# Expert weights of a mixture-of-experts layer on one Trainium2 core: three whole transfers per expert, or twelve of 32 partitions

## The chip, the core and the metric

The kernel runs on one core of one Trainium2 chip. The metric is the device time of one execution in microseconds. Durations of single instructions and stretches come from one profiled execution, whose times are counted from the start of its span.

## What is computed

One pre-norm transformer layer over 8 sequences of 512 tokens (4096 tokens of width 512). The first part is attention, half softmax attention and half a gated linear recurrence. The second part, which the change touches, is a mixture of 32 experts with a capacity of 160 slots each. Cut to what matters:

```python
C = int(math.ceil(CF * T / E))                   # 160 slots per expert
slots_token = jnp.zeros(EC, jnp.int32).at[dest].add(jnp.where(valid, tok_s, 0))
slots_w = jnp.zeros(EC, w_s.dtype).at[dest].add(jnp.where(valid, w_s, 0.0))
Xp = x[slots_token].reshape(E, C, d)             # E = 32, d = 512
G = jnp.einsum('ecd,edi->eci', Xp, W_gate)       # i = 256
U = jnp.einsum('ecd,edi->eci', Xp, W_up)
Y = jnp.einsum('eci,eid->ecd', jax.nn.silu(G) * U, W_down)
Yf = Y.reshape(EC, d) * slots_w[:, None]
out = jnp.zeros((T, d), x.dtype).at[slots_token].add(Yf)
return (out + shared).reshape(b, s, d)
```

Each expert has three float32 matrices of 512 KB: gate and up (512 x 256) and down (256 x 512).

## The kernel before, in words

The program has three phases, one behind the other.

**Attention** (to about 2077 us) doesn't meet the change.

**Routing and shared expert** (to about 2446 us) goes over eight blocks of 512 tokens. It picks the experts, scatters each token's row into a table `rows` in HBM with one indirect transfer per 128 tokens and pick (L1306, POOL), and writes the shared expert's result into the output. SP stores a block (L1268), loads the next one (L1238), and ahead of the store of block 5 issues the weights of the first five experts (L1262 to L1266), which nothing there needs yet.

**Experts** (`expert_phase`, from 2446 us) goes over the 32 experts. Each engine's order is written out by hand:

- SP loads the input rows of an expert (`load_x`, L1802: 160 rows of 528 values, on 80 partitions, into one of four tiles `xg`) and its weights (`load_expert`, L1099, into one of five sets of `held.room`). Weights of expert e + 1 wait until DVE has converted all three matrices of the expert that had the set before (`w_low`); inputs of expert e wait until PE has turned and POOL has read the expert that had the tile (`turned`, `share_ready`, L1800 and L1801).
- ACT converts gate, up and down to a high fp16 part (`up_high` L1855, `down_high` L1862), DVE to a low part (L1905). PE turns the inputs (L1952), multiplies by gate and up (L1965) and by down (L1978), each as three products of high and low parts.
- ACT scales the result by the slot's weight into one of four tiles `yo` (`copy_down`, L1881). POOL prepares that weight (`weigh`, L1822 to L1831) and adds the 160 rows to the output with two indirect accumulating transfers (`add`, L1840). Ahead of the two stands a wait until the previous expert's two have landed:

```python
for e in range(E_):
    if e + 2 < E_:
        weigh(e + 2)
    add(e)
```

```python
pool.wait_ge(share_ready, e + 1)
if e:
    pool.wait_ge(added, ONE_ADD * e)
pool.wait_ge(yo_ready, n_ct * (e + 1))
```

A weight matrix is laid on 128 partitions of 4 KB each, contiguous in HBM. All transfers but the indirect ones are issued by SP. The instructions that the change touches are `load_expert` and the two waits in `up_high` (L1856) and `down_high` (L1863).

Of the kernel before, what the change touches and what calls it, by code (L numbers as in the profile page):

```python
# [6 lines left out]
P = 128  # L7
# [1057 lines left out]
AT_SLOTS = AT_WEIGHTS + K  # L1065
ROW = DM + 16
SETS = 5


class Held:  # L1070


    def __init__(self, nc, ctx, cap):
        n_ct, ct = slot_tiles(cap)

        def sb(name, shape, dt=F32):
            return ctx.enter_context(nc.sbuf_tensor("held_" + name, shape, dt))

        self.room = sb("expert_w", [P, SETS, 3, DC * FF])
        self.ident = sb("ident", [P, P])  # L1080
        self.own = sb("own", [ct, n_ct, E_])
        self.up_loaded = [ctx.enter_context(nc.semaphore(f"expert_up_loaded{n}")) for n in range(SETS)]
        self.down_loaded = [ctx.enter_context(nc.semaphore(f"expert_down_loaded{n}")) for n in range(SETS)]

# [9 lines left out]
    def tail_room(self, n):  # L1094
        flat = self.room[:, SETS - 2:SETS, :, :].rearrange("p n m w -> p (n m w)")
        return flat[:, n * 4 * DM:(n + 1) * 4 * DM].rearrange("p (r d) -> p r d", d=DM)


def load_expert(eng, held, w_gate, w_up, w_down, e):  # L1099

    n = e % SETS
    eng.dma_start(held.gate(n), w_gate[e].rearrange("(p c) i -> p c i", p=P)).then_inc(held.up_loaded[n], 16)
    eng.dma_start(held.up(n), w_up[e].rearrange("(p c) i -> p c i", p=P)).then_inc(held.up_loaded[n], 16)
    eng.dma_start(held.down(n), w_down[e].rearrange("(p c) d -> p c d", p=P)).then_inc(held.down_loaded[n], 16)


def routing_phase(nc, x2, router_w, e_bias, shared_gate, shared_up, shared_down, consts, acc_dram, rows_dram, held,
# [10 lines left out]
    with ExitStack() as ctx:  # L1118
# [117 lines left out]
        def _(sp):  # L1236
# [25 lines left out]
            for b in range(B):  # L1262
                if b == max(B - 3, 0):
                    sp.wait_ge(w_ready, 12)
                    for e in range(SETS):
                        load_expert(sp, held, w_gate, w_up, w_down, e)  # L1266
                sp.wait_ge(summed, NT * (b + 1))
                sp.dma_start(acc_dram[b * SEQ:(b + 1) * SEQ, :].rearrange("(i p) d -> p i d", p=P), xr[b % RING][:]).then_inc(base_stored, 16)  # L1268
                if b + RING < B:
                    sp.wait_ge(base_stored, 16 * (b + 1))  # L1270
                    load_x(b + RING)
# [465 lines left out]
def expert_phase(nc, T, w, rows_dram, acc_dram, out, held):  # L1737
# [5 lines left out]
    w_gate, w_up, w_down = w  # L1743
    out_rows = out.rearrange("b t d -> (b t) d")
    with ExitStack() as ctx:
# [26 lines left out]
        def by_chunk(bank):  # L1772
            return bank[:, 0:FC * cap].rearrange("p (c t) -> p c t", c=FC)
# [22 lines left out]
        @block.sync  # L1796
        def _(sp):
            def load_x(e):
                if e >= XS:
                    sp.wait_ge(turned, n_ct * (e - XS + 1))  # L1800
                    sp.wait_ge(share_ready, e - XS + 1)  # L1801
                sp.dma_start(xg[e % XS][:], rows_dram[e * cap:(e + 1) * cap, :].rearrange("(j p) d -> p j d", p=ct)).then_inc(x_loaded[e % XS], 16)  # L1802

            for e in range(XS):
                load_x(e)
            for e in range(XS, E_):
                if e + 1 >= SETS and e + 1 < E_:
                    sp.wait_ge(w_low, 3 * (e + 1 - SETS + 1))
                    load_expert(sp, held, w_gate, w_up, w_down, e + 1)
                load_x(e)  # L1810
            sp.wait_ge(added, ONE_ADD * E_)
# [39 lines left out]
        @block.scalar  # L1851
        def _(act):
            act.preload_act_table_set("sigmoid_and_others")

            def up_high(e):  # L1855
                act.wait_ge(held.up_loaded[e % SETS], 32 * (e // SETS + 1))  # L1856
                if e >= 2:
                    act.wait_ge(up_done, e - 1)
                for whole, part in ((held.gate(e % SETS), wg_part), (held.up(e % SETS), wu_part)):
                    nc.scalar.activation(part[e % 2][0][:], whole, ACT.Copy, scale=W_SCALE).then_inc(w_high, 1)  # L1860

            def down_high(e):  # L1862
                act.wait_ge(held.down_loaded[e % SETS], 16 * (e // SETS + 1))  # L1863
                if e >= 2:
                    act.wait_ge(down_done, n_ct * (e - 1))
                nc.scalar.activation(wd_part[e % 2][0][:], held.down(e % SETS), ACT.Copy, scale=W_SCALE).then_inc(w_high, 1)

            def copy_turned(e):
                for j in range(n_ct):
                    act.wait_ge(turned, n_ct * e + j + 1)  # L1870
                    nc.scalar.activation(xp_t[e % 2][0][:, :, j * ct:(j + 1) * ct],
                                         tr_ps[j % 2][:, 0:DC * ct].rearrange("p (c t) -> p c t", c=DC),
                                         ACT.Copy, scale=X_SCALE).then_inc(x_high_ready, 1)

            def copy_down(e):
                act.wait_ge(share_ready, e + 1)
                if e >= XS:
                    act.wait_ge(added, ONE_ADD * (e - XS + 1))
                for j in range(n_ct):
                    act.wait_ge(down_done, n_ct * e + j + 1)  # L1880
                    nc.scalar.activation(yo[e % XS][:, j, :], down_ps[j % 2][0:ct, :], ACT.Copy,  # L1881
                                         scale=share[e % XS][:, j:j + 1]).then_inc(yo_ready, 1)

            up_high(0)
            copy_turned(0)
            for e in range(E_):
                down_high(e)
                if e + 1 < E_:
                    up_high(e + 1)
                    copy_turned(e + 1)  # L1890
                act.wait_ge(gate_done, e + 1)
                if e >= 2:
                    act.wait_ge(h_step, 2 * (e - 1))
                nc.scalar.activation(sig[e % 2][:], by_chunk(gate_ps[e % 2]), ACT.Sigmoid,
                                     scale=1.0 / (X_SCALE * W_SCALE)).then_inc(sig_ready, 1)
                if e:
                    copy_down(e - 1)
                act.wait_ge(h_step, 2 * (e + 1))
                nc.scalar.copy(h_part[e % 2][0][:], h[e % 2][:]).then_inc(h_high_ready, 1)
            copy_down(E_ - 1)  # L1900
# [172 lines left out]
```

## Time and profile before, and how to read it

| | |
|---|---|
| median of 3 runs | 2734.24 us (2732.66 to 2735.64) |
| the profiled execution | 2731.19 us |
| its span, first to last instruction | 2729.2 us |
| PE busy | 2533.8 us, 93% of the span |
| DVE, ACT, POOL busy | 1918.4, 1574.0, 1565.8 us |
| DMA, mean over the span | 52 GB/s, 143.23 MB |
| routing phase / expert phase | about 2077 to 2446 / 2446 to 2729 us |

The busy shares are means over three phases that have different limits; the change bears on the last 283 us and on a stretch from 2327 us. For that phase the views by stretch and by wait are the ones to read.

### The profile page before, as it was taken

The numbers are of one execution on the slowest core, as the hardware profiler recorded it, in microseconds if no ns is written. First come the engines' busy times: TensorE is split into PE (matmuls) and PEld (weight loads), VectorE is DVE, ScalarE is ACT, GpSimd is POOL, SyncE is SP. The second block draws the span as 40 slices with busy tenths as digits, with TensorE's granted clock in tenths as the row PEclk, the third lists the DMA queues.
The fourth block names the chain that finished last, engine by engine and source line by source line (L and its number), as shares of the span: only waits on it lengthen the run. The fifth ranks groups of instructions, "written<-read, shape, count | busy, mean of one in ns | idle before, by whom it ended". The sixth has DMA issues, their size and how long they took to land. (4 is left out here: it accounts for less than half of the span.)

```text
span 2729.2 us, 52852 instructions
## 1 busy us (share of the span) xinstructions
PE 2533.8 (93%) x16740; PEld 1729.4 (63%) x16740; DVE 1918.4 (70%) x4613; ACT 1574.0 (58%) x4789; POOL 1565.8 (57%) x2005
## 2 busy tenths in 40 slices
PE   5899999999999999999999999999996899979885
PEld 3666666666666666666666666666664444538764
DVE  7777677767776776777777777766764777647763
ACT  5656666666665655666666656655654333317664
POOL 4556556655665565566556655655541566655665
PEclk8999999999999999999999999999998999989998
DMA  5500000000000000000000000000003221427783
GB/s 177 191 1 17 30 3 1 17 32 1 2 17 32 1 17 17 17 1 17 32 1 2 17 32 1 2 5 28 1 1 113 91 80 36 165 60 257 258 254 73
DMA packets 68767, 143.23 MB, mean 52 GB/s; under 512 B 15863, under 2 KB 21239, under 8 KB 68304
## 3 DMA queue, kind: packets, MB, share of 16 engines
q1 hardware_dynamic: 52112, 128.39, 13.9%
q0 software_dynamic: 16384, 11.47, 2.2%
q8 instruction: 141, 2.31, 0.4%
q14 instruction: 130, 1.06, 0.1%
HBM read 111.60 MB, written 72.68 MB: 68 GB/s over the span
## 5 line engine op out<-in xcount | busy, mean ns | idle before, releaser
L303 POOL TENSOR_TENSOR parts<-qk,rope 128x640 f32<-128x640 f32 x128 | 197.4, 1542 | 441.2 <-issue 301.3
L437 ACT ACTIVATE prob<-score_ps,neg_max 128x512 f32<-128x512 f32 (+3 forms) x512 | 272.2, 532 | 249.7 <-DVE neg_max L630 213.2
L857 PE MATMUL out_ps<-prob_t,val 128*128 128x512 f32 (+3 forms) x1024 | 305.6, 442 | 14.4 <-ACT prob_t L443 10.3
L830 PE MATMUL score_ps<-kr_t,qr_t 128*128 128x512 f16 (+3 forms) x1536 | 284.1, 300 | 13.2 <-ACT prob L437 11.2
L638 DVE TENSOR_SCALAR prob<-prob,inv_sum 128x512 f32<-128x512 f32 (+3 forms) x512 | 273.5, 534 | 18.0
L857 PEld LDWEIGHTS out_ps<-prob_t,val 128*128 128x128 f32 x1024 | 185.2, 191 | 134.0 <-issue 62.1
L630 DVE TENSOR_REDUCE neg_max<-score_ps 128x1 f32<-128x512 f32 (+3 forms) x512 | 237.2, 483 | 25.9 <-PE score_ps L832 19.7
L479 ACT ACTIVATE soft<-qk,neg_top 128x128 f32<-128x128 f32 x640 | 247.1, 387 | 0.8
L343 POOL TENSOR_TENSOR k_dec<-decay,keys 128x32 f32<-128x32 f32 (+3 forms) x512 | 165.5, 355 | 83.1 <-ACT decay L499 83.1
L315 POOL TENSOR_TENSOR rot<-parts 128x320 f32<-128x320 f32 x128 | 110.9, 866 | 167.8 <-DVE parts L660 167.8
L636 DVE RECIPROCAL inv_sum<-row_sum 128x1 f32<-128x1 f32 x512 | 81.1, 158 | 175.5 <-ACT prob L437 175.4
L903 PE MATMUL qkv_ps<-wq_high,x_t_high 128*128 128x512 f16 x512 | 197.0, 385 | 2.0 <-DVE wkv_low L561 2.0
L903 PE MATMUL qkv_ps<-wq_low,x_t_high 128*128 128x512 f16 x512 | 196.9, 384 | 0.0
L903 PE MATMUL qkv_ps<-wq_high,x_t_low 128*128 128x512 f16 x512 | 196.7, 384 | 0.0
L356 POOL TENSOR_TENSOR o_t_low<-parts,o_t_high 128x512 f16<-128x512 f32 x128 | 148.1, 1157 | 75.1 <-ACT parts L453 75.1
L830 PEld LDWEIGHTS score_ps<-kr_t,qr_t 128*128 128x128 f16 x1536 | 135.5, 98 | 82.8 <-ACT prob L437 38.5
L321 POOL TENSOR_TENSOR soft<-soft,inv_tot 128x512 f32<-128x512 f32 x128 | 146.1, 1141 | 63.3 <-DVE inv_tot L672 63.3
L462 ACT ACTIVATE qk<-qkv_ps 128x640 f32<-128x640 f32 x128 | 90.1, 704 | 142.4 <-issue 127.7
L443 ACT COPY prob_t<-prob_ps 128x384 f32<-128x384 f32 (+1 forms) x256 | 94.6, 369 | 116.3 <-DVE prob_t L646 114.2
L1306 POOL DMA_INDIRECT rows<-r_yn,r_sk_i x128 | 129.2, 1009 | 53.8 <-issue 45.7
L1840 POOL DMA_INDIRECT out_dram<-e_yo,e_goal x64 | 107.7, 1683 | 89.5 <-issue 73.7
L332 POOL TENSOR_TENSOR decay<-keys 128x512 f32<-128x512 f32 x128 | 141.5, 1106 | 7.8 <-ACT keys L486 5.8
(294 smaller groups left out, 7807.2 us busy)
## 6 DMA issues: line engine op xcount, KB each, us to landing
held_expert_w<-in_L_ffn_W_gate_dram SPq DMA_DIRECT2D x32, 512.0 KB
held_expert_w<-in_L_ffn_W_up_dram SPq DMA_DIRECT2D x32, 512.0 KB
held_expert_w<-in_L_ffn_W_down_dram SPq DMA_DIRECT2D x32, 512.0 KB
rows<-const_empty_dram SPq DMA_DIRECT2D x1, 10560.0 KB, 39.7
e_xg<-rows SPq DMA_DIRECT2D x32, 330.0 KB, 4.9
x_in<-_attn_hidden_states_dram SPq DMA_DIRECT2D x8, 1024.0 KB, 5.5
x_acc<-_attn_hidden_states_dram SPq DMA_DIRECT2D x8, 1024.0 KB, 5.4
x<-x_acc SPq DMA_DIRECT2D x8, 1024.0 KB, 4.4
```

Of the source, the lines that this page charges most:

```text
L303: nc.gpsimd.tensor_tensor(parts[:, 1, :].rearrange("p (h d) -> p h d", d=HALF), qk[:].rearrange("p (h d) -> p h d", d=HALF), rope[:, i, 1: ...
L321: nc.gpsimd.tensor_tensor(q, q, inv_tot[:, 0:G].unsqueeze(2).to_broadcast([P, G, DH]), ALU.mult).then_inc(soft_query_ready, 1)
L332: nc.gpsimd.tensor_tensor(decay[:, 0:NSUB * P].rearrange("p (c s) -> p c s", s=P), mid.to_broadcast([P, NSUB, P]), run.unsqueeze(1).to_bro ...
L343: ins = nc.gpsimd.tensor_tensor(k_dec[:, s, 0:m], decay[:, s * P:s * P + m], keys[:, 0:m], ALU.mult)
L356: nc.gpsimd.tensor_tensor(o_t[1][:, h, :], o_whole, o_t[0][:, h, :], ALU.subtract).then_inc(o_t_ready, 1)
L437: nc.scalar.activation(prob[:, i % 2, 0:w], score_ps[i % 2][:, 0:w], ACT.Exp, bias=neg_max[:, j:j + 1], accum_out=row_sum[:, j:j + 1]).the ...
L479: ins = nc.scalar.activation(soft[:, h * DH:(h + 1) * DH], qk[:, h * DH:(h + 1) * DH], ACT.Exp, bias=neg_top[:, h:h + 1], accum_out=tot[:, ...
L630: nc.vector.tensor_reduce(neg_max[:, j:j + 1], score_ps[i % 2][:, 0:w], AX_X, ALU.max, negate=True).then_inc(max_ready, 1)
L638: nc.vector.tensor_scalar(prob[:, i % 2, 0:w], prob[:, i % 2, 0:w], inv_sum[:, j:j + 1], None, ALU.mult).then_inc(prob_ready, 1)
L830: nc.tensor.matmul(score_ps[i % 2][:, 0:w], qr_t[p][:, q_, h, i * P:(i + 1) * P], kr_t[p][:, k_, 0:w], start=(n == 0), stop=False)
L857: nc.tensor.matmul(out_ps[:, j * P:SEQ], val[p][:, j, :], prob_t[:, j, j * P:SEQ], start=(j == 0), stop=False, skip_group_check=True)
L903: ins = nc.tensor.matmul(qkv_ps[:, 0:G * DH], x_t[x_part][:, d, i * P:(i + 1) * P], wq[w][:, d, gn * G * DH:(gn + 1) * G * DH], start=(d = ...
```

## The change

Each of an expert's three transfers becomes four, of 32 partitions and 128 KB each. The pieces of gate and up alternate: gate 0, up 0, gate 1, up 1, and so on, and the four pieces of down follow. The semaphores `up_loaded` and `down_loaded` of a set now rise by 128 and 64 for one expert instead of 32 and 16, and the two waits of ACT ask for these sums. All of an expert's pieces are issued behind the same wait as before.

```diff
+PIECES = 4
...
 def load_expert(eng, held, w_gate, w_up, w_down, e):
 
     n = e % SETS
-    eng.dma_start(held.gate(n), w_gate[e].rearrange("(p c) i -> p c i", p=P)).then_inc(held.up_loaded[n], 16)
-    eng.dma_start(held.up(n), w_up[e].rearrange("(p c) i -> p c i", p=P)).then_inc(held.up_loaded[n], 16)
-    eng.dma_start(held.down(n), w_down[e].rearrange("(p c) d -> p c d", p=P)).then_inc(held.down_loaded[n], 16)
+    for q in range(PIECES):
+        at = slice(q * P // PIECES, (q + 1) * P // PIECES)
+        eng.dma_start(held.gate(n)[at], w_gate[e].rearrange("(p c) i -> p c i", p=P)[at]).then_inc(held.up_loaded[n], 16)
+        eng.dma_start(held.up(n)[at], w_up[e].rearrange("(p c) i -> p c i", p=P)[at]).then_inc(held.up_loaded[n], 16)
+    for q in range(PIECES):
+        at = slice(q * P // PIECES, (q + 1) * P // PIECES)
+        eng.dma_start(held.down(n)[at], w_down[e].rearrange("(p c) d -> p c d", p=P)[at]).then_inc(held.down_loaded[n], 16)
...
             def up_high(e):
-                act.wait_ge(held.up_loaded[e % SETS], 32 * (e // SETS + 1))
+                act.wait_ge(held.up_loaded[e % SETS], 32 * PIECES * (e // SETS + 1))
...
             def down_high(e):
-                act.wait_ge(held.down_loaded[e % SETS], 16 * (e // SETS + 1))
+                act.wait_ge(held.down_loaded[e % SETS], 16 * PIECES * (e // SETS + 1))
```

The order of SP's instructions in the middle of the expert phase, before (one expert's weights, the next input load, and the first weight of the following expert; `e_xg` is the input tile, 80x2x528 its partitions and row):

```order
L1102 DMA held_expert_w<-in_L0_ffn_W_gate_dram 128x1024 [waits e_w_low]
L1103 DMA held_expert_w<-in_L0_ffn_W_up_dram 128x1024
L1104 DMA held_expert_w<-in_L0_ffn_W_down_dram 128x1024
L1802 DMA e_xg1<-rows 80x2x528 [waits e_share_ready,e_turned]
L1102 DMA held_expert_w<-in_L0_ffn_W_gate_dram 128x1024 [waits e_w_low]
```

The same place of the changed program:

```order
L1105 DMA held_expert_w<-in_L0_ffn_W_gate_dram 32x1024 [waits e_w_low]
L1106 DMA held_expert_w<-in_L0_ffn_W_up_dram 32x1024
L1105 DMA held_expert_w<-in_L0_ffn_W_gate_dram 32x1024
L1106 DMA held_expert_w<-in_L0_ffn_W_up_dram 32x1024
L1105 DMA held_expert_w<-in_L0_ffn_W_gate_dram 32x1024
L1106 DMA held_expert_w<-in_L0_ffn_W_up_dram 32x1024
L1105 DMA held_expert_w<-in_L0_ffn_W_gate_dram 32x1024
L1106 DMA held_expert_w<-in_L0_ffn_W_up_dram 32x1024
L1109 DMA held_expert_w<-in_L0_ffn_W_down_dram 32x1024 x4
L1807 DMA e_xg0<-rows 80x2x528 [waits e_share_ready,e_turned]
L1105 DMA held_expert_w<-in_L0_ffn_W_gate_dram 32x1024 [waits e_w_low]
```

Between two input loads there are now twelve issues instead of three. The same holds in the routing phase, where sixty issues stand in front of the store of block 5 instead of fifteen. No instruction of the other engines moves.

## Rows read from the trace of the kernel before

**Rows 1.** The chain that ended last, in order of time: start, duration, what.
```profile
2714.45 1.42 DMA out_dram<-e_yo,e_goal
...
2720.93 1.42 POOL out_dram L1840
```

**Rows 2.** Waits, 2504 to 2670: waited for, us in total, times, longest.
```profile
POOL out_dram L1840 <- issue: 53.6, 40, 5.5
ACT e_yo L1881 <- POOL e_goal L1831: 41.4, 16, 3.7
```

**Rows 3.** POOL in order of time: scatters at the stretch's ends and the last.
```profile
2468.42 1.50 POOL L1840 DMA_INDIRECT out_dram<-e_yo,e_goal  x1 [10.18 <-ACT e_yo L1881]
...
2506.80 1.50 POOL L1840 DMA_INDIRECT out_dram<-e_yo,e_goal  x1 [5.55 <-issue]
...
2672.20 1.64 POOL L1840 DMA_INDIRECT out_dram<-e_yo,e_goal  x1 [3.66 <-issue]
...
2712.71 1.43 POOL L1840 DMA_INDIRECT out_dram<-e_yo,e_goal  x1 [3.35 <-issue]
...
2719.21 1.42 POOL L1840 DMA_INDIRECT out_dram<-e_yo,e_goal  x1 [3.35 <-issue]
```

**Rows 4.** The output's scatters, 2504 to 2672: issue to landing.
```profile
DMA to landing us min/median/max: 3.8/5.8/7.5
```

**Rows 5.** The same from 2676 us to the end.
```profile
DMA to landing us min/median/max: 2.5/3.9/5.0
```

**Rows 6.** Stretches: length, busy PE PEld DVE ACT POOL (instructions), clock, DMA share, GB/s.
```profile
2330.00:2350.00 20.00, 19.72 (x114) 11.06 (x115) 17.69 (x57) 11.23 (x20) 15.55 (x16) 0.91 1.04 403
2448.00:2452.00 4.00, 1.34 (x8) 1.10 (x8) 3.29 (x4) 2.85 (x5) 2.05 (x4) 0.50 1.04 253
...
2504.00:2664.00 160.00, 144.08 (x1379) 115.27 (x1377) 113.16 (x161) 108.77 (x181) 104.55 (x154) 0.99 0.80 249
```

**Rows 7.** SP in order of time: issues of weights and inputs.
```profile
2327.82 0.50 SPq L1102 DMA_DIRECT2D held_expert_w<-in_L_ffn_W_gate_dram  x1
...
2333.80 1.48 SPq L1104 DMA_DIRECT2D held_expert_w<-in_L_ffn_W_down_dram  x1
...
2363.50 78.41 SPq L1268 DMA_DIRECT2D out_dram<-r_xr  x3
...
2453.76 0.36 SPq L1102 DMA_DIRECT2D held_expert_w<-in_L_ffn_W_gate_dram  x1
...
2585.97 0.33 SPq L1802 DMA_DIRECT2D e_xg<-rows  x1
2586.34 0.44 SPq L1102 DMA_DIRECT2D held_expert_w<-in_L_ffn_W_gate_dram  x1
...
2587.31 0.43 SPq L1104 DMA_DIRECT2D held_expert_w<-in_L_ffn_W_down_dram  x1
```

**Rows 8.** What SP's queue waited for, 2504 to 2670.
```profile
SPq L1801 <- POOL e_goal L1831: 124.9, 20, 8.9
```

**Rows 9.** The router weights' transfer, 32 partitions, 64 KB: issue ns.
```profile
L1242 SPq DMA_DIRECT2D r_rw<-in_L_ffn_router_w_dram x1: 423/423/423, 2079.2 to 2079.2; - x1
```

**Rows 10.** ACT in order of time: first expert, and the last one.
```profile
2447.50 1.06 ACT L1860 ACTIVATE e_wg_high<-held_expert_w 128x1024 f16<-128x1024 f32 x1
...
2687.41 1.05 ACT L1860 ACTIVATE e_wg_high<-held_expert_w 128x1024 f16<-128x1024 f32 x1
...
2697.59 1.26 ACT L1881 ACTIVATE e_yo<-e_down_ps,e_share 80x512 f32<-80x512 f32 x2 [2.44 <-POOL e_goal L1831]
2698.75 0.45 ACT L1899 CAST e_h_high<-e_h 128x320 f16<-128x320 f32 x1
```

**Rows 11.** DMA issues of the page: KB each, median us to landing.
```profile
e_xg<-rows SPq DMA_DIRECT2D x32, 330.0 KB, 4.9
```

**Rows 12.** PE in order of time: first and last matmul of a down product.
```profile
2591.32 0.38 PE L1978 MATMUL e_down_ps<-e_wd_high,e_h_high 128*80 128x512 f16 x1
...
2593.69 0.38 PE L1978 MATMUL e_down_ps<-e_wd_high,e_h_low 128*80 128x512 f16 x1
```

## Prediction

> **What bounds the kernel now.** The change touches only the transfers of the expert weights, so I read the expert phase alone (from 2446 us) and asked what sets the pace of one expert there. First the end: the chain that ended last is the accumulating scatter into the output, the landing of one (2714.45) and then the issue of the next (2720.93), with nothing of the matrix engine in it [rows 1]. Then the waits of the steady stretch 2504 to 2670 us: POOL stands 53.6 us in front of its scatters (L1840) although no engine is named, and ACT stands 41.4 us in front of `yo` for the shares that POOL writes [rows 2]. In the code POOL waits at that place for the previous expert's scatters to have landed (`added`). Nobody in that stretch waits for weights. Third, POOL in order of time [rows 3]: the first scatter of one expert starts at 2506.80 and that of the expert twenty later at 2672.20, so one expert takes 165.4 / 20 = 8.27 us. At the end, with no weights in flight, two such starts (2712.71 and 2719.21) are 6.50 us apart. The difference is the landing: issue to landing has a median of 5.8 us in the stretch with weight traffic and 3.9 us behind it [rows 4, 5]. So the expert phase is a chain of 32 experts' scatters, and the DMA traffic beside them sets its pace.
>
> Fourth, the DMA engines by stretch [rows 6]. Five experts' weights, all on 128 partitions, move in 2330 to 2350 at 403 GB/s with the engines fully busy (share 1.04; above 1, packets overlap). In 2448 to 2452 the queue holds the first expert inputs, which have 80 partitions, and the engines are as busy (1.04) but move only 253 GB/s. That is the row this forecast rests on: 253 / 403 = 0.63, and 80 / 128 is 0.63. In the steady stretch the share is 0.80. Last, SP [rows 7]: an expert is one input issue and three weight issues, at a pitch of 0.48 us, and SP then waits 124.9 / 20 = 6.2 us per expert for POOL [rows 8].
>
> **The change, part by part.**
>
> *Issues.* Three issues per expert become twelve; nine more at the pitch of 0.485 us (2586.34 to 2587.31, two steps [rows 7]) are 4.4 us, out of the 6.2 us that SP waits. A 32-partition transfer of before was issued in 423 ns [rows 9], no cheaper and no dearer than a 128-partition one. SP then needs 12 x 0.485 + 0.37 = 6.2 us of 8.27 us: free. Behind these issues on SP stands the next input load (L1802), which lands 4.4 us later at worst; by the code its tile is used two experts (16 us) later. Free as well. The semaphore sums change from 32 and 16 to 128 and 64 per round, with the same waits at the same places of ACT.
>
> *Prefetch in the routing phase.* Sixty issues (29 us) from 2327.82; SP is next wanted at 2363.50 [rows 7]. 7.86 MB take 20 us at 403 GB/s and 39 us at half of it, until 2367 us, and the first use is at 2447.5 [rows 10]: covered by 80 us. POOL's row scatters run beside it for longer; between 0 and 3 us, I take 0.
>
> *The rate of a piece.* All of it hangs on this. A piece writes 32 partitions where a whole transfer wrote 128; bytes and row size (4 KB) are the same. No large 32-partition transfer is in the trace, so I bound it. At one end the partitions don't matter: 403 GB/s, 1.573 MB in 3.9 us per expert. At the other the rate falls with the number of partitions, as it does between 128 and 80: 403 / 4 = 101 GB/s, 15.6 us. I take half, 202 GB/s and 7.8 us, the geometric middle; the row at 80 partitions excludes for me that nothing happens, and a load in which sixteen engines still take part is unlikely to fall to a quarter.
>
> The Trainium skill (SBUF — State Buffer, Door 1: The DMA port swizzle) says that a transfer reaches only the ports its own partitions belong to, 8 of 16 for partitions 0 to 31, and gives 189 GB/s at 1 MiB and about 218 GB/s at best; by it the weights of one expert would be an estimated 7.2 to 8.3 us. By that rule 80 partitions reach full width only for a part of their bytes, with which the 253 GB/s agree. The same page's "Can I just issue two DMAs to hit both halves?" says that pieces on different halves gain only 6% from each other, which speaks against this change.
>
> *DMA demand per expert.* Weights 7.8 us. The input, 0.338 MB (330 KB, [rows 11]) at 253 GB/s, 1.35 us. The scatters: now 0.80 x 8.27 = 6.6 us of engine time per expert, less 3.9 and 1.35, leaves 1.35, say 1.4 us. Sum 7.8 + 1.35 + 1.4 = 10.5 us, above the 8.27 us of today: the DMA engines become the pace.
>
> *Where that ends.* From the weights' side: the first load in the expert phase is issued at 2453.76 [rows 7]; 27 experts at 10.5 us are 284 us; from the last landing to the end I count 24 us: 11.3 from the last expert's first conversion to its product (2687.41 to 2698.75), less the 2.4 in which ACT waited for POOL, the down product 2.7 (2591.32 to 2593.69, and one matmul), `yo` 1.3 [rows 10, 12], 10.0 from its first scatter to the end, and 1 for the landing. 2453.8 + 283.5 + 24 = 2761 us, 32 us over the span of 2729.2. From the scatters' side: first scatter at 2468.42 [rows 3], 27 steps at 10.5, four at 6.5 behind the last weights, 10.0 from the last expert's first scatter to the end: 2468.4 + 283.5 + 26 + 10 = 2788 us, 59 us over. The scatter chain starts slow if the weights don't hold it up yet, so I take the middle, **+45 us**. Time of the profiled execution 2731.19 + 45 = 2776; it lies 3.05 below the median of the three runs, so against those it is **2780 us**.
>
> Bounds of the same term. At 403 GB/s the sum is 3.9 + 1.35 + 1.4 = 6.65 us, below 8.27: nothing. At 253 GB/s, 8.95 us: 27 x 0.68 = +18 us. From the landing: weight traffic at a share of 0.80 costs 5.8 - 3.9 = 1.9 us; if it is always there, and each piece in the way takes twice as long, 1.9 / 0.80 x 2 = 4.75 us on top of 6.50, a step of 11.25 us and 2468.4 + 304 + 36 = 2808 us, +79.
>
> **The rivals.**
>
> *The pieces move as fast as before.* Then weights are landed some 20 us before use as now, SP has room, and the time stays at 2734. For it: the sixteen engines may drift apart, so that some write one piece and some the next; the bytes are the same. Against: the 80-partition row. Chance 0.15.
>
> *Faster: the issues pace the traffic.* This needs the rate to stay near 403 GB/s. Today three issues put 1.57 MB into the queue in 1.5 us, and a scatter that meets it lands up to 7.5 us later [rows 4]. Twelve issues spread the same bytes over 5.8 us, 270 GB/s, leaving a third of the engines free at any moment; the 1.9 us of delay would shrink by a third, 20 steps x 0.6 = -12 us, 2722 us. It decides once pieces run above about 270 GB/s. The Trainium skill (Perfetto Trace Analysis, DMA Optimizations) says that splitting may let transfers start sooner where the DMA engines are generally idle; here they are busy for 0.80 of the time. Chance 0.08.
>
> *SP becomes the bound.* With a full queue issues took up to 1.48 us each [rows 7]. At about 1.1 us for each piece, an expert is 12 x 1.1 + 0.37 = 13.6 us: 2453.8 + 367 + 24 = 2845, about 2850 us. Against: those slow issues drained 512 KB each, pieces are a quarter. Chance 0.05.
>
> *The rate falls to a quarter.* 15.6 + 2.75 = 18.3 us per expert: 2453.8 + 494 + 24 = 2972, about 2977 us. Chance 0.07.
>
> That the change doesn't split at all is excluded: the instruction order shows pieces of 32 partitions.
>
> **How the numbers follow.** The forecast case, slower by 10 to 95 us around 2780, has 0.65. No change 0.15, faster 0.08, the two dear cases 0.12. The measurement can tell about 0.2%, 5.5 us. Faster by more than that 0.08, within it 0.15, slower 0.65 + 0.12 = 0.77. The range leaves out the fast rival and the two dear ones, 0.20 together: from 2729, the no-change case's lower edge, to 2830, the +79 bound and some 15 us for a slower drain. The forecast's own range is 2745 to 2830.
>
> **What would show it.** In the changed profile: the stretch 2330 to 2350 at about 200 GB/s with a share of 1.0, the weights landing past 2360; in the expert phase a share near 1.0 and less than 230 GB/s; a step of 10 us or more between experts' first scatters; ACT waiting for weight transfers at L1865; scatter landing median 7 us or more. I am wrong if 2330 to 2350 still shows 400 GB/s, or if it shows 200 and the expert phase still keeps 8.3 us, which would mean that the scatters' landing, not the engines' capacity, is what matters. SP waiting for nothing at all would be the third rival.

## The result, and the profile after

The change makes the kernel slower: 2765.16 us (median of 4 runs, 2763.88 to 2766.46) against 2733.66 us (4 runs), a ratio of 1.0119 with a 95% interval of 1.0106 to 1.0132, or +31.5 us. 2780 was forecast, with a range of 2729 to 2830. The profiled execution has a span of 2764.4 us, 35.2 more than before.

One stretch of the prefetch, before:

```profile
2338.00:2350.00 12.00, 12.00 (x58) 6.06 (x58) 11.13 (x47) 6.76 (x12) 8.75 (x9) 0.86 1.04 399
```

The same stretch of the kernel after, and one of its expert phase (columns as in [rows 6]):

```profile
2338.00:2350.00 12.00, 12.00 (x73) 7.47 (x72) 11.21 (x37) 6.03 (x11) 8.10 (x8) 1.00 1.06 230
2504.00:2664.00 160.00, 131.23 (x1195) 103.69 (x1193) 96.73 (x137) 91.91 (x153) 83.24 (x136) 0.95 1.01 223
```

In the prefetch the DMA engines are as busy as before (1.06) and move 230 GB/s instead of 399. The last row answers to 0.80 and 249 GB/s: in the expert phase the engines are now busy all the time and bring fewer bytes, and PE's busy time falls from 144 to 131 us of 160.

POOL in order of time, the scatters that open an expert's step:

```profile
2471.04 1.50 POOL L1845 DMA_INDIRECT out_dram<-e_yo,e_goal  x1 [10.40 <-ACT e_yo L1886]
...
2506.73 1.76 POOL L1845 DMA_INDIRECT out_dram<-e_yo,e_goal  x1 [5.32 <-issue]
...
2698.14 2.51 POOL L1845 DMA_INDIRECT out_dram<-e_yo,e_goal  x1 [5.07 <-issue]
...
2754.48 1.41 POOL L1845 DMA_INDIRECT out_dram<-e_yo,e_goal  x1 [3.29 <-issue]
```

From 2506.73 to 2698.14 are twenty steps, from the fourth expert to the 24th: 9.57 us each. The same twenty steps took 8.36 us before. The 8.27 us of [rows 3] are those from the fifth expert to the 25th, and these take 9.41 us now. The span's 35.2 us can be read off these times. The first scatter is 2.6 us late. Most of that is older than the change, since the first weight issue already comes 2.4 us later than before (2330.19 against 2327.82, [rows 7]). From the first scatter to the fourth expert's it is 35.7 us against 26.4 (+9.3), over the next twenty steps 191.4 against 167.3 (+24.1), and over the last eight, of which only the first still has weights beside it, 56.3 against 57.1 (-0.8). In the first stretch, 2465 to 2504 us, the median landing of the scatters is 9.4 us where it was 5.1, so the early steps lose by the same wait.

The waits of the same stretch as in [rows 2], 2504 to 2690 us, and below them what SP's queue waited for:

```profile
POOL out_dram L1845 <- issue: 89.8, 39, 7.0
ACT e_yo L1886 <- POOL e_goal L1836: 76.4, 19, 6.4
DVE e_h_low L1946 <- ACT e_h_high L1904: 62.0, 20, 5.6
```

```profile
SPq L1806 <- POOL e_goal L1836: 58.9, 19, 5.6
```

The same waits as before have grown: POOL in front of its scatters, ACT for POOL's shares. No row names a weight transfer. SP still waits for POOL, 3.1 us per expert where it was 6.2 [rows 8]. The landing of the scatters, 2504 to 2700 us:

```profile
DMA to landing us min/median/max: 4.5/6.8/9.9
```

5.8 has become 6.8 us [rows 4]. Behind the weight traffic the median is 3.9 us in both.

### The profile page after: what moved, and what is told of

Read it like the earlier page. It is cut to its first block and busy times, and to the rows that moved or that the text cites. A ratio compares the mean times of both kernels' runs of the same rounds, so it can differ in the third digit from the quotient of the medians.

```text
span 2764.4 us, 53140 instructions
## 1 busy us (share of the span) xinstructions
PE 2551.7 (92%) x16740; PEld 1739.5 (63%) x16740; DVE 1918.7 (69%) x4613; ACT 1571.8 (57%) x4789; POOL 1552.9 (56%) x2005
## 5 line engine op out<-in xcount | busy, mean ns | idle before, releaser
L499 ACT ACTIVATE decay<-decay 128x640 f32<-128x640 f32 x128 | 96.6, 754 | 85.0 <-POOL decay L335 85.0
```

## The experiments

All are built on the changed kernel unless said otherwise. Each was built to tell between theories. Theory A: a transfer's rate depends on which partitions it writes, and 32 neighbours reach half the width. B: the number of transfers costs. C: the number of partitions in a transfer sets its rate. D: the step grows with the slow transfers smoothly, against a threshold of the engines' capacity.

### Every fourth partition

```diff
-        at = slice(q * P // PIECES, (q + 1) * P // PIECES)
+        at = slice(q, P, PIECES)
```

> Twelve pieces of 32 partitions and 4 KB rows as in the change, but piece q takes partitions q, q+4, q+8 and so on over all 128. Theory A (a piece of neighbouring partitions reaches only half of the write width): the prefetch stretch moves 380 to 400 GB/s again instead of 227, the step between experts' first scatters is 7.8 to 8.4 us instead of 9.57, the time 2722 to 2740 us. Theory B (the number of transfers costs, by their fixed work on the engines) and theory C (the number of partitions in one transfer sets its rate): 227 GB/s, 9.6 us, about 2765 us.

Measured: 2736.23 us (2732.9 to 2742.73), ratio 1.0015 (1.0006 to 1.0024). Its prefetch stretch, and SP's issues of gate:

```profile
2338.00:2350.00 12.00, 12.00 (x65) 7.00 (x64) 11.18 (x37) 5.90 (x10) 8.57 (x9) 0.86 0.71 208
```

```profile
L1105 SPq DMA_DIRECT2D held_expert_w<-in_L_ffn_W_gate_dram x128: 468/594/1752, 2329.5 to 2685.8; - x128
```

The time is what A expected, the rate is not: 208 GB/s. But the engines are busy for only 0.71 of it, where the change's pieces had them at 1.06 for 230 GB/s. What limits here is the issue, 594 ns a piece instead of 422: 131 KB in about 0.64 us are 205 GB/s. So the same bytes, rows and count of pieces take clearly less engine time once a piece is spread over all partitions, and B and C fall. They are not as cheap as whole transfers: 0.71 for 208 GB/s is 31% more engine time per byte than 1.04 for 399. The issue shows in the expert phase too, 2504 to 2664 us:

```profile
PEld e_tr_ps L1957 <- DMA e_xg<-rows: 22.8, 15, 3.5
PE e_tr_ps L1957 <- DMA e_xg<-rows: 19.8, 14, 3.3
```

PE waits for inputs, which stand behind the twelve issues on SP, and SP itself has no wait left in that stretch. The scatters land in 5.0 us (the row below, 2504 to 2664 us), but SP's twelve issues set a step of 8.30 us (fifth expert to 25th). The third rival of the prediction happens here, in another kernel than the one it was for.

```profile
DMA to landing us min/median/max: 3.2/5.0/6.8
```

### Two halves

```diff
-PIECES = 4
+PIECES = 2
```

> Two pieces per matrix, partitions 0 to 63 and 64 to 127, six transfers per expert. Theory A: each still reaches half the width, so 220 to 235 GB/s in the prefetch and about 2765 us. Theory B: half of the added transfers, so half of the loss of time per byte, about 290 GB/s and 2745 to 2750 us. Theory C: twice the partitions of a piece, clearly above 227 GB/s (about 300), 2740 to 2750 us.

Measured: 2765.45 us, ratio 1.0114 (1.0099 to 1.0130), that is the changed kernel's time.

```profile
2338.00:2350.00 12.00, 12.00 (x66) 7.06 (x65) 11.18 (x38) 5.90 (x10) 8.45 (x9) 0.86 1.05 233
```

64 neighbouring partitions move at 233 GB/s and 32 at 230. Half the number of transfers gains nothing (against B), twice the partitions gain nothing (against C). Whole transfers on 128 move at 403.

The Trainium skill (SBUF — State Buffer, Door 1: The DMA port swizzle) gives 189 GB/s for partitions 0 to 31 and 196 for 0 to 63 at 1 MiB; by that rule, 8 ports of 16 for both, the runs agree in the equality, and lie some 20% above its figures. They also lie 6% over the 218 GB/s that the prediction quotes from it as the best.

### The order of the sides

Three runs change nothing but the order of the twelve pieces.

```diff
-    for q in range(PIECES):
+    for q in (0, 2, 1, 3):
```

> The twelve pieces of the change, issued in the order of partitions 0-31, 64-95, 32-63, 96-127, so that pieces that follow each other lie on different sides of partition 64 (gate and up of the same partitions still follow each other). Theory A, if the engines overlap pieces that follow each other: above 227 GB/s, 240 to 300, and 2745 to 2760 us; if they keep step: 227 GB/s and 2765 us. Theories B and C: 227 GB/s and 2765 us.

The second issues the four pieces of gate, then the four of up, in order:

```diff
     for q in range(PIECES):
         at = slice(q * P // PIECES, (q + 1) * P // PIECES)
         eng.dma_start(held.gate(n)[at], ...
+    for q in range(PIECES):
+        at = slice(q * P // PIECES, (q + 1) * P // PIECES)
         eng.dma_start(held.up(n)[at], ...
```

> The pieces of the change, but the four of gate first, then the four of up: two pieces below partition 64 are followed by two above, instead of four by four. The alternation of gate and up itself is worth nothing since nobody waits for weights. Theory A with overlap of neighbours: a gain from the more frequent change of side as in the run with the order 0, 2, 1, 3, which had the same pattern for gate and up, 2748 to 2756 us. Without overlap: 2765 us.

The third does both, so that every piece is followed by one from the other side of partition 64.

> Gate, then up, then down, each in the order 0-31, 64-95, 32-63, 96-127: every piece is followed by one on the other side of partition 64. Theory A with overlap: more overlap than with pairs, 260 GB/s or more in the prefetch, 2735 to 2748 us. If the 2750 us of the pairs was the most that overlap gives: 2750 us.

Measured: 2749.6 us (ratio 1.0065, 1.0049 to 1.0081), 2757.53 (1.0093, 1.0078 to 1.0108) and 2743.59 (1.0038, 1.0024 to 1.0053). The prefetch stretch of the first, the second and the third:

```profile
2338.00:2350.00 12.00, 12.00 (x50) 5.15 (x49) 11.28 (x38) 5.09 (x9) 9.70 (x9) 0.89 1.06 243
```

```profile
2338.00:2350.00 12.00, 12.00 (x69) 6.81 (x69) 11.14 (x47) 6.82 (x12) 8.43 (x10) 1.00 1.05 232
```

```profile
2338.00:2350.00 12.00, 12.00 (x67) 6.58 (x67) 11.11 (x48) 7.01 (x12) 8.70 (x9) 1.00 1.06 251
```

The more often the side of partition 64 changes, the lower the time (2765, 2758, 2750, 2744). The rate rises from 230 to 243 and 251 GB/s in the first and third; in the second, where the side changes only every two pieces, it is 232. What differs is the order of the pieces, so A holds once more, and neighbours on the queue overlap a little, 9% at most. The rates of the last run fell short of the 260 expected; the time was inside. The second run was put a little too low (2748 to 2756); I had left out that its down pieces keep their order. The alternation of gate and up, which is what it undoes, costs some 6 or 7 us of the 31.5 (1.0119 against 1.0093, with intervals that just meet); with it four pieces in a row write the same side.

### Cut by columns

```diff
-        eng.dma_start(held.gate(n)[at], w_gate[e].rearrange("(p c) i -> p c i", p=P)[at]).then_inc(held.up_loaded[n], 16)
+        eng.dma_start(held.gate(n)[:, q, :], w_gate[e].rearrange("(p c) i -> p c i", p=P)[:, q, :]).then_inc(held.up_loaded[n], 16)
```

(up and down likewise, each piece 128 partitions by 1 KB.)

> Twelve pieces of 128 KB per expert, each on all 128 partitions with a row of 1 KB instead of 4 KB (the matrices cut by columns of the tile). Theory A: 330 to 400 GB/s in the prefetch and 2730 to 2745 us, the small loss by the shorter rows. Theory B: 227 GB/s or less and 2765 us or more. Theory C: as A.

Measured: 2734.28 us (10 runs), ratio 1.0003 (0.9994 to 1.0013): no loss.

```profile
2338.00:2350.00 12.00, 12.00 (x66) 7.07 (x65) 11.18 (x39) 6.61 (x11) 8.14 (x9) 0.86 0.92 282
```

282 GB/s is below the 330 expected. A piece was issued in 432 ns; with the gap between issues that is about 0.47 us, which allows 279 GB/s: here too SP paces the prefetch. Twelve transfers per expert as such cost no time: B falls for good. They do occupy the engines longer, 0.93 of the expert phase instead of 0.80.

One rival to A was not tested. A matrix's row lies in HBM where its partition says, so every piece of neighbouring partitions also reads one contiguous block of HBM, and the strided and column pieces read from all over the matrix. What speaks against HBM as the cause is that pieces taken in turn from two matrices on the same side moved no faster (230 GB/s, the change) than pieces from one (232 GB/s, gate and then up), while a change of side did raise the rate.

### Part of the weights only

Down alone in pieces (gate and up whole, their wait sum 32 again):

```diff
+    eng.dma_start(held.gate(n), ...).then_inc(held.up_loaded[n], 16)
+    eng.dma_start(held.up(n), ...).then_inc(held.up_loaded[n], 16)
     for q in range(PIECES):
         ... held.down(n)[at] ...
```

> Only the down matrix goes in four pieces of 32 neighbouring partitions; gate and up go whole. Theory A with the engines' capacity as the pace (a step takes the sum of the engine time of an expert's weights, input and scatters): 2 x 1.3 + 2.3 + 1.35 + 1.4 = 7.6 us, below today's 8.27, so no loss, 2731 to 2738 us. Rival D (the scatters land later in proportion to how long slow pieces are under way, whatever the sum): a third of the loss, about +10 us, 2743 us.

Gate and up alone in pieces, down whole (its wait sum 16 again):

```diff
     for q in range(PIECES):
         ... held.gate(n)[at] ... held.up(n)[at] ...
+    eng.dma_start(held.down(n), ...).then_inc(held.down_loaded[n], 16)
```

> Only gate and up go in pieces, down goes whole. Capacity: 4.6 + 1.3 + 1.35 + 1.4 = 8.65 us, 0.4 above 8.27, so 27 x 0.4 = +10, 2740 to 2748 us. Rival D: two thirds of the loss, +21 us, 2754 us.

The pieces for the first five experts alone (`if e < SETS:`, whole transfers behind it):

> The pieces of the change for the first five experts alone, which are loaded in the routing phase; all later ones whole. If the routing phase covers the slow loads as forecast: 2731 to 2738 us. If the slow prefetch costs something itself (row scatters of POOL held up, store of block 5 behind sixty issues): up to the whole 32 us.

Measured: down alone 2741.69 us, ratio 1.0042 (1.0029 to 1.0056), +11.5; gate and up alone 2756.24, 1.0092 (1.0078 to 1.0105), +26; prefetch alone 2731.41, 1.0002 (0.9993 to 1.0011). The expert phase of the first, and the landing of its scatters:

```profile
2504.00:2664.00 160.00, 138.66 (x1283) 111.61 (x1282) 104.56 (x150) 100.18 (x166) 98.20 (x151) 0.96 0.88 238
...
DMA to landing us min/median/max: 2.9/6.1/8.1
```

Slow pieces in the prefetch are free, as forecast, though they fill the engines there:

```profile
2338.00:2350.00 12.00, 12.00 (x65) 7.04 (x64) 11.21 (x38) 6.84 (x11) 8.14 (x9) 0.86 1.06 230
```

In the expert phase there is no threshold for such pieces. With down alone the engines have 12% of their time free and the sum I had taken as the pace lies under 8.27 us, yet 11.5 us are lost, a good third of the whole. Rival D holds (it gave 2743 and 2754 us), and the capacity rule falls.

### Less traffic

From the kernel before, with the weight transfers of experts 5 to 31 cut to a row of 512 B:

```diff
+    eng.dma_start(held.gate(n)[:, 0, 0:FF // 2], ...[:, 0, 0:FF // 2]).then_inc(held.up_loaded[n], 16)
```

> The kernel before, whose weight transfers in the expert phase (experts 5 to 31) bring only one eighth of each matrix, a row of 512 B on all 128 partitions; the rest of the weights is left out. It shows the pace of the scatter chain with hardly any weight traffic. If the traffic sets the landing as I say: scatters land in about 4 us instead of 5.8, the step falls from 8.27 to 6.9 to 7.4 us, the time to 2700 to 2712 us. If the chain has a pace of its own: above 2725 us.

From the changed kernel, pieces with half of each row for experts 5 to 31:

```diff
-        eng.dma_start(held.gate(n)[at], ...[at]).then_inc(held.up_loaded[n], 16)
+        eng.dma_start(held.gate(n)[at, 0:2], ...[at, 0:2]).then_inc(held.up_loaded[n], 16)
```

> The twelve pieces of the change with only the first half of each row (2 KB) for experts 5 to 31; the other half of these weights is left out. The bytes are half, the engine time of an expert's weights is 786 KB / 227 GB/s = 3.5 us, near the 3.9 us of the whole transfers. Theory D' (the scatters' delay follows the time for which weight transfers occupy the engines): as before, 2723 to 2732 us. If it follows the bytes: halfway between the eighth (2706) and before, 2714 to 2720 us. If it follows the lower rate as such (each packet of a piece in the way takes twice as long): 2745 us or more.

Measured: 2705.67 us (0.9911, 0.9896 to 0.9926) and 2719.33 us (0.9952, 0.9937 to 0.9967). Both leave weights out and are no improvements. First the run with an eighth, then the one with half rows:

```profile
2504.00:2664.00 160.00, 159.40 (x1569) 130.44 (x1567) 130.68 (x185) 129.72 (x207) 131.75 (x178) 1.00 0.45 92
...
DMA to landing us min/median/max: 2.6/4.0/5.1
```

```profile
2504.00:2664.00 160.00, 152.44 (x1480) 122.25 (x1478) 124.19 (x176) 119.04 (x195) 122.03 (x167) 1.00 0.71 165
...
DMA to landing us min/median/max: 2.6/4.5/6.5
```

With an eighth of the weights the step falls to 7.24 us and 24.5 us come back: the weights cost the kernel before 24.5 us by delaying the scatters, though nobody waits for them. The scatters are no longer what sets the pace in that run. PE is busy 159.4 of 160 us, and POOL stands only 23.0 us in front of 44 scatters (53.6 us for 40 before), so still earlier landings would gain little. The half-row run came out at -12.5 us, in the range of "follows the bytes", and refuted the third reading, by which the low rate itself would double each delay (2745). It doesn't separate the other two: I had put the engine time of its weights 0.4 us below that of whole transfers (3.5 against 3.9), but its share of 0.71 over a step of 7.82 us is 5.6 us per expert, about 1 below the kernel before (0.80 x 8.27 = 6.6), so less time was occupied as well. Bytes alone can't be the rule all the same, since the change moves the same bytes as before and lost 31.5 us. With the measured shares, engine time per expert and time of the kernel go together:

| pieces | share x step, us | landing, us | time against before, us |
|---|---|---|---|
| an eighth of the weights | 0.45 x 7.24 = 3.3 | 4.0 | -24.5 |
| half rows | 0.71 x 7.82 = 5.6 | 4.5 | -12.5 |
| before | 0.80 x 8.27 = 6.6 | 5.8 | 0 |
| every fourth partition | 0.86 x 8.30 = 7.1 | 5.0 | +3 |
| columns | 0.93 x 8.33 = 7.7 | 5.5 | +1 |
| gate and up every fourth, down whole (below) | 0.93 x 8.21 = 7.6 | 5.4 | +2 |
| down alone | 0.88 x 8.62 = 7.6 | 6.1 | +11.5 |
| sides in turn | 0.95 x 8.48 = 8.1 | 5.8 | +12 |
| gate and up alone | 0.99 x 9.09 = 9.0 | 6.3 | +26 |
| two halves | 1.00 x 9.45 = 9.45 | 7.1 | +32.5 |
| the change | 1.01 x 9.41 = 9.5 | 6.7 | +31.5 |

(The step is the mean from the fifth expert's first scatter to the 25th's; share and landing are those of 2504 to 2664 us; the time is against the runs of before beside it.) Two cautions. Where the share is 1, share times step is the step itself, so those rows don't show by how much engine time delays a scatter. And the landing column leaves out the steps ahead of 2504 us, where from a third to over a half of the loss lies: from the first expert to the fifth the change lost 9.8 us, sides in turn 6.6, down alone 6.1, columns 3.2.

The runs whose pieces lie on all partitions stand out, by columns and with gate and up on every fourth: as much engine time as with down alone, and next to no loss. The scatters read `yo` on partitions 0 to 79; whether slow pieces on the same side as these hold them up more than others was not tried, and stays open.

### A try to gain from it

The strided run had the scatters land in 5.0 us and failed by SP's issues. With gate and up so cut and down whole (its wait sum 16 again) SP has room:

```diff
-        at = slice(q * P // PIECES, (q + 1) * P // PIECES)
+        at = slice(q, P, PIECES)
...
+    eng.dma_start(held.down(n), w_down[e].rearrange("(p c) d -> p c d", p=P)).then_inc(held.down_loaded[n], 16)
```

> Gate and up in four pieces each of every fourth partition, down whole: nine issues per expert. In the run with all three matrices cut that way SP never waited and its twelve issues of 594 ns set the step (8.38 us) while the scatters landed in 5.0 us. Here SP needs 8 x 0.64 + 0.48 + 0.37 = 6.0 us and has room again. If the scatter chain then profits from the paced traffic: landing about 5.2 us, step 7.7 to 7.9, 2718 to 2728 us. If the landing goes by the bytes alone: 2730 to 2736 us.

Measured: 2733.78 us (12 runs), ratio 1.0011 (1.0003 to 1.0020). That is in the range of "by the bytes alone", and not in that of a gain. The landing fell to 5.4 us and SP waits 36.5 us again, but the step stayed at 8.21 us. Why the earlier landing gained nothing is open. No version with all the weights beat the kernel before.

```profile
2504.00:2664.00 160.00, 146.56 (x1401) 118.00 (x1399) 114.07 (x161) 109.38 (x181) 110.95 (x159) 0.98 0.93 257
```

## Why the prediction was right, and where it was not

**What bounds the kernel: right.** The chain of scatters sets the pace of the expert phase, and DMA traffic sets the pace of the chain. The run with an eighth of the weights shows it: 24.5 us less, with the landing at 4.0 us, until PE's own work is the pace.

**The rate of a piece: right in kind, a little too low.** I took half, 202 GB/s; it was 230 GB/s. The two ends of the bound were far off on both sides (403 and 101). The row at 80 partitions had carried the right sign; that its rate fell as its width was a coincidence, as the equal rates of 32 and 64 show: width alone doesn't set it. With 230 GB/s an expert's weights take 6.8 us instead of 7.8, and the sum would have been 9.6 us, which the measured steps of 9.4 to 9.6 meet. The other two terms, 2.75 us together, hold as well: with an eighth of the weights the engines were occupied 3.3 us per expert, of which the weights at 403 GB/s are an estimated 0.5.

**"The DMA engines become the pace": wrong as a rule.** The sum fits the changed kernel, where the engines are full. But the step of the prediction by which nothing is lost below 8.27 us failed: with down alone the sum is 7.6 us and 11.5 us were lost. What the runs showed in its place is that engine time added below the limit already delays the scatters. By the table a microsecond more per expert costs the kernel 8 to 12 us when it comes from pieces on neighbouring partitions (31.5 / (9.5 - 6.6) = 11 for the change), and 1 or 2 us when the pieces lie on all partitions and SP has room. That difference the sum doesn't have at all, and its cause is open.

**Where it ends: the weights' side was no path.** I averaged 2761 us from the weights' landing and 2788 from the scatters. No engine ever waited for weights, contrary to the sign I had named at L1865, so only the scatter side counts. It was too long because its 27 steps were put at 10.5 us. Measured they take 257.1 us (2471.04 to 2728.13), 9.52 each, and 2788 - 26 = 2762 would have met the span of 2764.4. They are not equal, though: four of 10.7 to 13.1 us, twenty of 9.4 in the mean and three of 6.0 to 7.3. That 9.6 fits all of them is in part luck. The average of the two sides hid part of the error in the rate. The signs that I had put highest, a step of 10 us or more and a landing of 7 us, were both just missed (9.57 and 6.8).

**Issues and prefetch: right.** Nine more issues at 0.47 us left SP 3.1 us of waiting per expert, and the prefetch alone in pieces costs nothing that can be measured (ratio 1.0002, 0.9993 to 1.0011). The prefetch now fills the engines until about 2371 us, 4 us later than forecast, and 79 us before it is used.

**The rivals.** Pieces as fast as before: excluded by 230 GB/s. Faster by paced traffic: it needs pieces that keep their rate, and where these were made (by columns, every fourth partition) the landing did fall, to 5.5 and 5.4 us, but nothing was gained. SP as the bound: not in this kernel, but in the strided one. A quarter of the rate: excluded.

## What to carry to other kernels

Cut a transfer along the free dimension, not into groups of neighbouring partitions: 32 or 64 neighbours moved at 230 GB/s where 128 moved at 403, and the engines were no less busy. A transfer nobody waits for is still not free: here the scatters landed in 3.9 us without weights beside them, in 5.8 with whole ones and in 6.8 with pieces, and as they form the chain that sets the pace, that was paid even before the engines were full. Where the wait table shows POOL in front of an indirect transfer with no engine named, compare the landing time in a stretch with and without bulk traffic before touching anything else.

## What was not expected of the hardware

The time for which SP issues one transfer depends on its partitions in a way that its size does not explain: 32 neighbours 422 ns, all 128 432 ns (whole or by columns), but 64 neighbours 596 ns and 32 strided by four 594 ns. Twelve issues of the last kind fill an expert's step. The issue rows of gate in the changed kernel (min/median/max ns) and in the run with two halves:

```profile
L1105 SPq DMA_DIRECT2D held_expert_w<-in_L_ffn_W_gate_dram x128: 311/422/1689, 2330.2 to 2696.3; - x128
```

```profile
L1105 SPq DMA_DIRECT2D held_expert_w<-in_L_ffn_W_gate_dram x64: 465/596/1512, 2329.7 to 2697.2; - x64
```

The cause is open.
